# Four attention layers on one core: mixing constants added by ScalarE in PSUM, loads reordered, two results kept in PSUM

## The chip, the cores and the metric

The kernel runs on 1 core of one Trainium2 chip. The metric is the device time of one execution in microseconds (us), median of several runs, lower is better. The core has TensorE (PE, matmuls, results always in PSUM), VectorE (DVE), ScalarE (ACT), GpSimd (POOL) and SyncE (SP, which here only issues DMAs). In the profile PEld is TensorE's weight load, and "SPq", "DVEq" and the like are an engine's queue (issue, drains, waits) as against its datapath.

## What is computed

32 sequences of 64 tokens with 256 channels pass through four layers, all in f32. The reference, cut to its outline:

```python
x = L0(ctx, x, mask)       # attention of x over [ctx, x], 16 heads; rmsnorm; gelu MLP 256-1024-256
x = L1(x, state=ctx)       # layer norm, token shift, five mixes, linear recurrence over time, gated norm; then a second token-shift block
x = L2(x, ctx, masks)      # self attention, cross attention over ctx, gelu MLP 256-1024-256
x = L3(x, ctx, mask)       # cross attention over ctx, tanh(gate) * result added

# inside L1, the part the change touches
sx  = shift(xa) - xa
t   = tanh((xa + sx * maa_x) @ maa_w1)                  # five groups of 32 columns
m_j = t_j @ maa_w2[j]                                   # j = w, k, v, r, g
x_j = xa + sx * (maa_j + m_j)                           # the five mixes
...                                                     # r, k, v, g, decay from x_j; recurrence; y
y   = norm(y) * gn_w + gn_b;  x = x + (y * silu(g_proj)) @ Wo.T
x   = x + sigmoid(xr2 @ fWr.T) * (relu(xk2 @ fWk.T)**2 @ fWv.T)
```

## The kernel before, in words

The batch is cut into 8 groups of 4 sequences (256 tokens). A group lives in a "lane", one of four arenas in SBUF; lane i works through group i and then group i + 4. So four groups are under way at any time, each in one of the stages a (layer 0), b (first block of layer 1), c (second block of layer 1 and the self attention) and d (cross attention, MLP, layer 3). "First pass" below is groups 0 to 3, "second pass" groups 4 to 7.

Each engine runs one fixed instruction sequence. It is cut into steps, and the table `ORDER` says for each engine from which lane the next step comes: a string of digits, one digit a step (`P` is the prologue, on SP the loads of weights). A second table `BANKS` gives each PSUM tile one of the 8 banks. Both tables come from a planner outside the file. An engine never looks ahead: a step that waits blocks all that stands behind it.

The steps that matter here, with the lines of the kernel before:

- **Mixes** (`v_b`, line 993). For each of the five mixes PE fills a bank with t_j @ maa_w2[j] (line 622); DVE computes (bank + constant) * sx with two `scalar_tensor_tensor` instructions of 128x256, one for each half of the channels, into one of two slots of `L.mixed`; POOL adds xa (line 1482); PE runs the projection (lines 378 and 639). Mix n may overwrite its slot once projection n - 2 is done.
- **Recurrence** (`v_b`, `steps`): DVE multiplies in PSUM (line 1009), runs two scans (1013) and then a drain (1016) that hands the bank back; POOL multiplies by r (1492).
- **Gated norm** (lines 1057 and 1060): DVE multiplies the bank `rstd_rows` with `L.yc` in SBUF, result to SBUF, and hands the bank back at once; two more instructions of 128x256 read that result and make `L.yT`, on which PE waits (line 399).
- **End of layer 1** (lines 1083 and 1085): DVE computes (rr + 1) * bank `fv` into SBUF and hands the bank back, then adds half of it to x with an instruction of 128x512 whose two tensors both lie in SBUF.
- **Softmax of layer 0**: PE scores (543, 550), DVE maximum (940), ACT exp (1249), DVE sum and reciprocal (928, 930), POOL normalises (1420), PE transposes (366), ACT copies (1186), PE weights (571). POOL also makes the masks (1452), and adds the row constant to the residual x once x has been loaded (1458).
- **Loads**: SP issues, before anything else waits, the inputs of all four lanes, the weights `w_am`, the masks, the weights `w_b`, `w_c` and `w_d`, and only then the four residuals x (1566).

## Time and profile before

| what | value |
|---|---|
| median of 3 runs | 1033.16 us (1030.88 to 1034.33) |
| the profiled execution's own time | 1040.02 us |
| its span, first to last instruction | 1037.9 us |
| mean granted TensorE clock | 0.979 of full speed |
| busy: PE, DVE, ACT, POOL | 960.1, 742.7, 572.7, 543.3 us |
| weight loads of PE | 764.5 us |

The profiled execution took 6.9 us more than the median of the runs; all durations below are from that execution. Busy times are of one engine each and overlap freely. A matmul's end is modelled, so a busy PE is not a PE at its peak. "Idle before <- X" in a row is the time in which the engine stood still, put down to the instruction whose semaphore came last.

### The profile page before, as it was taken

Reading aid. Unit: us, or ns where it says so; the run is one execution under the profiler, and the core shown is the slowest. Engines: PE = TensorE matmul, PEld = TensorE weight load, DVE = VectorE, ACT = ScalarE, POOL = GpSimd, SP = SyncE. Lnnn points to the kernel's source line nnn. Section 1 sums busy time; section 2 is a strip of 40 time slices with the busy share of each in tenths; the row PEclk is TensorE's granted clock in tenths of the full one; section 3 lists DMA queues with packets and bytes.
Section 4 is the critical chain, followed back from the end, with each engine's and each line's share of the span. In section 5 each row is a group of like instructions: output and inputs, shape, how many; then the busy total and the mean of one; then the engine's idle time right before and its main releaser. Section 6 shows DMA issues by size and latency. Waiting matters only on the chain.

```text
span 1037.9 us, 27518 instructions
## 1 busy us (share of the span) xinstructions
PE 960.1 (92%) x10944; PEld 764.5 (74%) x10944; DVE 742.7 (72%) x1607; ACT 572.7 (55%) x1320; POOL 543.3 (52%) x662
## 2 busy tenths in 40 slices
PE   6979999989789999889999999998998999899997
PEld 4657886856567877668887788776767777688885
DVE  1485566788997788973756765676889887986675
ACT  2489733432333755667746587644545452575573
POOL 2364353574754456774426633555565664675341
PEclk9999999998897999999999999999999999999999
DMA  9601111000001001020101001101001000000001
GB/s 346 274 2 30 29 29 28 2 1 2 2 1 33 1 2 28 3 65 2 29 27 34 27 2 29 29 2 27 2 1 29 14 1 2 13 9 6 13 2 43
DMA packets 28589, 31.71 MB, mean 31 GB/s; under 512 B 14736, under 2 KB 25264, under 8 KB 27824
## 3 DMA queue, kind: packets, MB, share of 16 engines
q1 hardware_dynamic: 27440, 28.12, 8.4%
q8 instruction: 88, 1.44, 0.6%
q10 hardware_dynamic: 1024, 1.85, 0.5%
q14 instruction: 37, 0.30, 0.1%
HBM read 27.86 MB, written 2.10 MB: 29 GB/s over the span
## 4 chain that ended last, share of the span: by engine, by line
PE 53%; DVE 19%; DVEq 9%; issue 7%; ACT 5%; POOL 4%; POOLq 2%; DMA 1%; ACTq 0%; SPq 0%
PE bank L494 8%; PE bank L506 7%; PE bank L378 6%; PE bank L366 5%; PE bank L399 5%; PE bank L391 3%; DVE lane L1013 3%; DVEq L1016 3%; DVE bank L1009 2%; PE bank L457 2%; DVEq L886 2%; PE bank L481 2%; DVE lane L865 2%; PE bank L524 2%; PE bank L535 2%
## 5 line engine op out<-in xcount | busy, mean ns | idle before, releaser
L1420 POOL TENSOR_TENSOR lane<-lane 128x512 f32<-128x512 f32 x160 | 167.8, 1052 | 159.1 <-DVE lane L887 90.8
L1186 ACT COPY lane<-bank 128x512 f32<-128x512 f32 x232 | 132.0, 590 | 166.8 <-PE bank L366 103.9
L366 PE MATMUL bank<-ident,lane 128*128 128x128 f32 x896 | 131.9, 282 | 16.4 <-POOL lane L1420 4.5
L366 PEld LDWEIGHTS bank<-ident,lane 128*128 128x128 f32 x896 | 102.7, 143 | 42.8 <-issue 14.8
L1492 POOL TENSOR_TENSOR lane<-lane 128x512 f32<-128x512 f32 x64 | 81.3, 1271 | 70.1 <-DVE lane L1013 69.8
L1013 DVE TENSOR_TENSOR_SCAN lane<-lane,bank 128x256 f32<-128x256 f32 x128 | 80.9, 674 | 5.0 <-issue 0.4
L1205 ACT ACTIVATE lane<-lane 128x512 f32<-128x512 f32 x96 | 60.3, 633 | 28.9 <-DVE lane L865 28.5
L1154 ACT ACTIVATE lane<-lane 128x256 f32<-128x256 f32 x96 | 52.3, 594 | 42.4 <-POOL lane L1405 42.0
L885 DVE TENSOR_REDUCE lane<-lane 128x8 f32<-128x512 f32 x96 | 64.8, 675 | 12.1 <-ACT lane L1205 11.7
L1217 ACT ACTIVATE lane<-bank,vecs 128x256 f32<-128x256 f32 x128 | 51.9, 477 | 36.6 <-PE bank L494 36.3
L1168 ACT ACTIVATE lane<-bank,vecs 128x256 f32<-128x256 f32 x112 | 55.3, 550 | 22.9 <-PE bank L366 22.5
L1482 POOL TENSOR_TENSOR lane<-lane 128x512 f32<-128x512 f32 x40 | 46.8, 1180 | 39.2 <-DVE lane L993 39.2
L378 PE MATMUL bank<-lane,w_b 128*128 128x256 f32 x256 | 64.3, 398 | 2.9 <-POOL lane L1482 2.7
L506 PE MATMUL bank<-w_d,lane 128*128 128x256 f32 x256 | 61.6, 382 | 0.5 <-ACTq L1253 0.5
L506 PE MATMUL bank<-w_am,lane 128*128 128x256 f32 x256 | 61.2, 382 | 0.0
L494 PE MATMUL bank<-lane,w_d 128*128 128x256 f32 x256 | 59.1, 382 | 0.9 <-DVEq L1016 0.9
L494 PE MATMUL bank<-lane,w_am 128*128 128x256 f32 x256 | 58.8, 382 | 0.9 <-DVE lane L865 0.8
L378 PEld LDWEIGHTS bank<-lane,w_b 128*128 128x128 f32 x256 | 48.5, 197 | 14.2 <-POOL lane L1482 4.8
L816 DVE TENSOR_TENSOR lane<-bank,lane 128x512 f32<-128x512 f32 x48 | 33.0, 687 | 34.2 <-PE bank L399 23.8
L1179 ACT ACTIVATE lane<-bank,scalars 128x256 f32<-128x256 f32 x64 | 31.3, 540 | 46.3 <-PE bank L391 46.0
L1009 DVE TENSOR_TENSOR bank<-bank,lane 128x512 f32<-128x512 f32 x64 | 44.5, 695 | 17.1 <-PE bank L668 11.9
L494 PEld LDWEIGHTS bank<-lane,w_d 128*128 128x128 f32 x256 | 47.4, 190 | 8.5 <-DVEq L1016 1.3
(161 smaller groups left out, 2243.4 us busy)
## 6 DMA issues: line engine op xcount, KB each, us to landing
lane<-in_inT SPq DMA_DIRECT2D x16, 256.0 KB, 4.5
lane<-in_x SPq DMA_DIRECT2D x16, 256.0 KB, 2.9
w_d<-in_w_d SPq DMA_DIRECT2D x1, 3072.0 KB, 25.1
w_am<-in_w_am SPq DMA_DIRECT2D x1, 2048.0 KB, 15.5
lane<-in_inT SPq DMA_DIRECT2D x16, 128.0 KB, 3.0
lane<-in_ctx SPq DMA_DIRECT2D x8, 256.0 KB, 2.9
out_x<-lane SPq DMA_DIRECT2D x8, 256.0 KB, 2.2
w_c<-in_w_c SPq DMA_DIRECT2D x1, 1792.0 KB, 20.3
```

The lines of the kernel that those rows point to most:

```text
L366: ins = pe.transpose(t[:, i * P:(i + 1) * P], src, ident[:, :])
L378: ins = pe.matmul(o, w[:, ct, m * P:(m + 1) * P], r, start=(ct == 0), stop=(ct == CT - 1))
L494: ins = pe.matmul(t[:, i * T:(i + 1) * T], w1[:, ct, (2 * m + i) * P:(2 * m + i + 1) * P], xnT[:, ct, :], start=(ct == 0), stop=(ct == CT ...
L506: ins = pe.matmul(t[:, tt * C:(tt + 1) * C], hidden[k][:, tt * P:(tt + 1) * P], w2[:, k, :], start=(k == 0), stop=(k == FT - 1))
L885: v.tensor_reduce(A.den[:, j, :], grid(A.probs[j]), AX_X, ALU.add)
L1009: v.tensor_tensor(kv, kv, L.bk[:, m, :, 0:S].unsqueeze(1).to_broadcast([P, 2, G, S]), ALU.mult)
L1013: ins = v.tensor_tensor_scan(st[:, e, :, :].rearrange("p b t -> p (b t)"), w, bk.tile(key)[:, e * T:(e + 1) * T], 0.0, ALU.mult, ALU.add)
L1168: ins = s.activation(o, src, ACT.Identity, scale=vec(scale, ct), bias=vec(shift, ct) if shift else 0.0)
L1186: s.copy(out, src).then_inc(bk.free_sem(key), 1)
L1205: s.activation(A.probs[step], A.probs[step], ACT.Exp).then_inc(sig["probs"].sem, 1)
L1420: p.tensor_tensor(q, q, den.unsqueeze(2).to_broadcast([P, n, 512 // n]), ALU.mult).then_inc(sig["normal"].sem, 1)
L1492: p.tensor_tensor(st, st, L.br[:, m, :].unsqueeze(1).to_broadcast([P, 2, T]), ALU.mult).then_inc(sig["rs"].sem, 1)
```

## The change

**Mixes.** After PE has filled a mix's bank, ACT adds the constant in place: two `activation` instructions (Identity, with a bias per partition) of 128x256 that read and write the same bank. It signals a new semaphore `shares`. DVE waits for `shares` and multiplies the whole bank with sx in one `tensor_tensor` of 128x512. The POOL step and the projection stay as they are. ACT's steps for mixes 0 and 1 come ahead of its tanh of the decay projection, those of mixes 2 to 4 behind it, each a step of its own.

**Gated norm.** The product of `rstd_rows` and `L.yc` is written back into the bank; the two instructions that make `L.yT` read it there. The bank is handed back after them, by a drain that is new.

**End of layer 1.** (rr + 1) * `fv` is written back into the bank, the last instruction reads it there and hands the bank back.

**Loads.** The four residuals are issued ahead of the weights `w_am`, `w_b`, `w_c`, `w_d`. SP waits for all four residuals to have landed before it issues `w_b`; and by the new order it has by then also issued the second loads of x of lanes 1 and 0, each of which waits for that lane's norm of layer 0.

**Order and banks.** `ORDER` and `BANKS` are new throughout, on all engines. The semaphore `bias` is merged into `x_bias`.

```diff
@@ v_b, the mixes
                 if n >= 2:
                     v.wait_ge(bk.full_sem((g, "proj", MIXES[n - 2][0])), bk.full_at((g, "proj", MIXES[n - 2][0])))
-                for ct in range(CT):
-                    ins = v.scalar_tensor_tensor(L.mixed[:, (n + 1) % 2, ct, :], t[:, ct * T:(ct + 1) * T], vec(name, ct), L.sx[:, ct, :],
-                                                 ALU.add, ALU.mult)
-                ins.then_inc(bk.free_sem(key), 1)
+                v.wait_ge(sig["shares"].sem, sig["shares"].at(g, n + 1))
+                v.tensor_tensor(flat(L.mixed[:, (n + 1) % 2, :, :]), t[:, :], flat(L.sx[:, :, :]), ALU.mult).then_inc(bk.free_sem(key), 1)
@@ v_b, the gated norm
-            v.scalar_tensor_tensor(flat(L.yc[:, :, :]), bk.tile(key)[:, :], 0.5, flat(L.yc[:, :, :]), ALU.mult, ALU.mult).then_inc(bk.free_sem(key), 1)
+            t = bk.tile(key)[:, :]
+            v.scalar_tensor_tensor(t, t, 0.5, flat(L.yc[:, :, :]), ALU.mult, ALU.mult)
             v.drain()
             for m in range(CT):
-                ins = v.scalar_tensor_tensor(L.yT[:, m, :], L.yc[:, m, :], gnb_half[:, m:m + 1], L.gate[:, m, :], ALU.add, ALU.mult)
+                ins = v.scalar_tensor_tensor(L.yT[:, m, :], t[:, m * T:(m + 1) * T], gnb_half[:, m:m + 1], L.gate[:, m, :], ALU.add, ALU.mult)
             ins.then_inc(sig["yT"].sem, 1)
+            v.drain().then_inc(bk.free_sem(key), 1)
@@ v_c, the end of layer 1
-            v.scalar_tensor_tensor(flat(L.rr), flat(L.rr), 1.0, bk.tile(key)[:, :], ALU.add, ALU.mult).then_inc(bk.free_sem(key), 1)
+            t = bk.tile(key)[:, :]
+            v.scalar_tensor_tensor(t, flat(L.rr), 1.0, t, ALU.add, ALU.mult)
             v.drain()
-            v.scalar_tensor_tensor(flat(x[:, :, :]), flat(L.rr), 0.5, flat(x[:, :, :]), ALU.mult, ALU.add)
+            v.scalar_tensor_tensor(flat(x[:, :, :]), t, 0.5, flat(x[:, :, :]), ALU.mult, ALU.add).then_inc(bk.free_sem(key), 1)
@@ s_b
+            def share(n):
+                key = (g, "mix", MIXES[n][0])
+                s.wait_ge(bk.full_sem(key), bk.full_at(key))
+                t = bk.tile(key)
+                for ct in range(CT):
+                    ins = s.activation(t[:, ct * T:(ct + 1) * T], t[:, ct * T:(ct + 1) * T], ACT.Identity, bias=vec(MIXES[n][0], ct))
+                ins.then_inc(sig["shares"].sem, 1)
@@ sp_weights
             sp.dma_start(wt["am"][:, :], a["w_am"]).then_inc(load["am"].sem, 16)
             yield
+            for g in range(NL):
+                sp.wait_ge(lane(g).sig["x_loaded"].sem, lane(g).sig["x_loaded"].at(g, 1))
             sp.dma_start(wt["b"][:, :], a["w_b"]).then_inc(load["b"].sem, 16)
@@ ORDER
     "SP": (
-        "0123P0123PPP001122330123000000112202222331111213333302131203"
+        "0112021120023333P10P2PP3010210000111321021222333332301230123"
```

What SP issues first. Before, the weights `w_am`, `w_b` and the rest stand ahead of the residuals (`in_x`), the first of which is here:

```order
L1548 DMA lane3<-in_inT 128x512 x2
L1589 DMA w_am<-in_w_am 128x4096
L1560 DMA lane0<-in_mask0 128x256
L1560 DMA lane1<-in_mask0 128x256
L1560 DMA lane2<-in_mask0 128x256
L1560 DMA lane3<-in_mask0 128x256
L1591 DMA w_b<-in_w_b 128x3264
L1592 DMA lora_w2<-in_maa_w2g 32x256
L1594 DMA decay_w2<-in_decay_w2 64x256 x2
L1595 DMA consts<-in_consts 128x1028
L1597 DMA w_c<-in_w_c 128x3584
```

The change's SP, from the tenth DMA on (line numbers are the change's own):

```order
L1581 DMA lane0<-in_x 128x2x256
L1581 DMA lane2<-in_x 128x2x256
L1563 DMA lane3<-in_inT 128x512 x2
L1575 DMA lane3<-in_mask0 128x256
L1577 DMA lane3<-in_b_small 128x16
L1581 DMA lane3<-in_x 128x2x256
L1604 DMA w_am<-in_w_am 128x4096
L1584 DMA lane1<-in_x 128x2x256
```

So all residuals go out ahead of `w_am`, and `w_b` to `w_d` come after steps that wait for a norm. On PE the first 47 us of work are nearly the same in both orders: the queries, keys and values of all four lanes and the first scores of lanes 0 and 1 stand ahead of the first transpose (line 366) in either.

DVE, the mixes of group 0 in the kernel before (the last three of five, and what follows):

```order
L993 SCALAR_TENSOR_TENSOR lane0<-bank6,vecs,lane0 128x256 x2
L993 SCALAR_TENSOR_TENSOR lane0<-bank3,vecs,lane0 128x256 x2
L993 SCALAR_TENSOR_TENSOR lane0<-bank7,vecs,lane0 128x256 x2
L851 TENSOR_SCALAR lane3<-bank3,vecs 128x128
L816 TENSOR_TENSOR lane3<-bank2,lane3 128x512
```

The same place in the change:

```order
L851 TENSOR_SCALAR lane3<-bank7,vecs 128x128
L993 TENSOR_TENSOR lane0<-bank3,lane0 128x512
L940 TENSOR_REDUCE lane3<-bank4 128x4
L993 TENSOR_TENSOR lane0<-bank6,lane0 128x512
L993 TENSOR_TENSOR lane0<-bank2,lane0 128x512
L949 TENSOR_SCALAR lane2<-lane2 128x256 x2
```

Each pair has become one instruction, and here a softmax row of lane 3 has moved in between. On ACT the new rows of the same group (line 1287 of the change), between lane 3's softmax and the next steps of lane 0:

```order
L1276 ACTIVATE lane0<-bank1 128x256
L1277 ACTIVATE lane0<-bank1 32x256
L1280 ACTIVATE scalars<-scalars 128x1
L1287 ACTIVATE bank2<-bank2,vecs 128x256 x2
L1287 ACTIVATE bank6<-bank6,vecs 128x256 x2
L1250 ACTIVATE lane3<-bank7,lane3 128x128 x4
L1187 COPY lane3<-bank3 128x512
L1295 ACTIVATE lane0<-bank6 128x128
L1250 ACTIVATE lane3<-bank1,lane3 128x128 x4
L1259 ACTIVATE lane2<-lane2 128x256 x2
L1287 ACTIVATE bank3<-bank3,vecs 128x256 x2
L1287 ACTIVATE bank6<-bank6,vecs 128x256 x2
```

Behind the ACT rows of a mix stand exps and copies of other lanes, which wait with it.

Three counts from the orders that no short piece shows. ACT's table loads are 47 before and 45 in the change. Stage b of a pass, counted from the first lane's `maa_w1` matmul (line 607 before) to the last lane's matmul on `head_scale` (line 724 before), spans 882 PE instructions of 6017 in the first pass before and 946 in the change; in the second pass it spans 1872 before and 1162 in the change. On DVE the same stage of the second pass spans 535 of 1608 instructions before and 377 of 1568 in the change.

## Rows read from the trace of the kernel before

**Rows 1.** Page: busy us (share of span) and instructions.
```profile
PE 960.1 (92%) x10944; PEld 764.5 (74%) x10944; DVE 742.7 (72%) x1607; ACT 572.7 (55%) x1320; POOL 543.3 (52%) x662
```
**Rows 2.** Stretches: PE, PEld, DVE, ACT, POOL busy (count), granted clock, DMA share, GB/s.
```profile
0.00:50.00 50.00, 40.83 (x208) 28.52 (x208) 14.50 (x32) 18.89 (x42) 14.31 (x24) 1.00 0.85 321
50.00:90.00 40.00, 30.38 (x576) 24.98 (x577) 33.28 (x74) 34.79 (x109) 25.48 (x27) 0.96 0.09 21
200.00:350.00 150.00, 131.28 (x1166) 98.38 (x1165) 131.71 (x273) 55.52 (x105) 90.45 (x104) 0.90 0.02 7
450.00:700.00 250.00, 246.55 (x2726) 200.31 (x2727) 152.97 (x345) 161.05 (x410) 123.17 (x149) 1.00 0.08 22
700.00:900.00 200.00, 182.58 (x2053) 141.84 (x2052) 166.52 (x357) 100.12 (x237) 120.32 (x149) 0.98 0.04 10
```
**Rows 3.** Timeline of POOL, start and duration, with the idle before.
```profile
43.52 1.27 POOL L1458 TENSOR_TENSOR lane<-lane,rows 128x512 f32<-128x512 f32 x1 [15.44 <-DMA lane<-in_x]
44.74 2.04 POOL L1420 TENSOR_TENSOR lane<-lane 128x512 f32<-128x512 f32 x2
46.74 3.72 POOL L1458 TENSOR_TENSOR lane<-lane,rows 128x512 f32<-128x512 f32 x3
```
**Rows 4.** Stretch 47 to 56, columns as in rows 2.
```profile
47.00:56.00 9.00, 6.09 (x98) 4.86 (x96) 5.72 (x13) 6.33 (x22) 8.45 (x8) 1.00 0.01 3
```
**Rows 5.** Chain that ended last, 255 to 300: start, us, what.
```profile
264.24 0.57 DVEq L1058
...
268.73 0.69 DVE lane L1013
269.42 0.58 DVEq L1016
270.00 0.14 issue
270.13 1.66 DVE lane L993 x4
271.79 0.60 DVE lane L816
```
**Rows 6.** Groups of instructions: count, busy us, mean ns, idle before and its releasers.
```profile
L993 DVE SCALAR_TENSOR_TENSOR lane<-bank,vecs,lane 128x256 f32<-128x256 f32 x80 | 34.2, 478 | 24.6 <-PE bank L622 15.8 <-PE bank L378 8.6
L816 DVE TENSOR_TENSOR lane<-bank,lane 128x512 f32<-128x512 f32 x48 | 33.0, 687 | 34.2 <-PE bank L399 23.8 <-PE bank L506 9.8 <-issue 0.6
L1009 DVE TENSOR_TENSOR bank<-bank,lane 128x512 f32<-128x512 f32 x64 | 44.5, 695 | 17.1 <-PE bank L668 11.9 <-issue 4.1
L1083 DVE SCALAR_TENSOR_TENSOR lane<-lane,bank 128x512 f32<-128x512 f32 x8 | 5.5, 682 | 0.5 <-PE bank L399 0.3 <-issue 0.2
L1217 ACT ACTIVATE lane<-bank,vecs 128x256 f32<-128x256 f32 x128 | 51.9, 477 | 36.6 <-PE bank L494 36.3
L1168 ACT ACTIVATE lane<-bank,vecs 128x256 f32<-128x256 f32 x112 | 55.3, 550 | 22.9 <-PE bank L366 22.5
```
**Rows 7.** DVE busy in line 1085 alone, 200 to 350 and 700 to 900.
```profile
200.00:350.00 150.00, 1.59 (x2) 0.90 0.02 7
...
700.00:900.00 200.00, 3.27 (x3) 0.98 0.04 10
```
**Rows 8.** DVE busy in line 1060 alone, the same stretches.
```profile
200.00:350.00 150.00, 2.64 (x6) 0.90 0.02 7
...
700.00:900.00 200.00, 3.58 (x6) 0.98 0.04 10
```
**Rows 9.** Who PE waited for: us in total, times, longest.
```profile
PE bank L378 <- POOL lane L1482: 2.7, 6, 0.9
...
PE bank L639 <- POOL lane L1482: 1.2, 1, 1.2
```
**Rows 10.** Stretches of stage b, columns as in rows 2.
```profile
120.00:330.00 210.00, 189.45 (x1533) 142.65 (x1532) 163.45 (x329) 76.64 (x162) 113.31 (x126) 0.93 0.04 12
560.00:880.00 320.00, 304.50 (x3263) 240.26 (x3262) 239.88 (x519) 178.25 (x453) 177.57 (x213) 0.99 0.05 13
```

More of the change, by code:

```diff
@@ L118 @@
+        "222333333323333330110221102233033"
     ),
     "SP": (
[L120 removed]
+        "0112021120023333P10P2PP3010210000111321021222333332301230123"
     ),
@@ L1118, in v_d @@
             yield
-            v.wait_ge(sig["bias"].sem, sig["bias"].at(g, BIAS["m"]))
+            v.wait_ge(sig["x_bias"].sem, sig["x_bias"].at(g, BIAS["m"]))
             v_add_rows(v, (g, "mm", "rows"), x)
@@ L1280, in s_b @@
             yield
+            def share(n):
[5 more added lines that the diff above has]
+                ins.then_inc(sig["shares"].sem, 1)
+            for n in range(2):
+                share(n)
+                yield
             key = (g, "proj", "maa_w")
@@ L1284, in s_b @@
             yield
+            for n in range(2, 5):
+                share(n)
+                yield
             s_copy(s, (g, "proj", "maa_k"), L.bk[:, :, :, 1:S + 1].rearrange("p m b t -> p (m b) t"), grid(bk.tile((g, "proj", "maa_k"))[:, :]))
@@ L1412, in p_bias @@
             p.wait_ge(sig["normed"].sem, sig["normed"].at(g, NORM[tag]))
-            p.tensor_tensor(L.x, L.x, row(name).unsqueeze(1).to_broadcast([P, TT, C]), ALU.add).then_inc(sig["bias"].sem, 1)
+            p.tensor_tensor(L.x, L.x, row(name).unsqueeze(1).to_broadcast([P, TT, C]), ALU.add).then_inc(sig["x_bias"].sem, 1)
         def p_normal(p, g, tag, j, probs, den, n):
```

85 lines of the change are left out of this document (42 added, 43 removed).

## The prediction, made before the changed kernel was run

> **What bounds the kernel now.** I read the page's busy times first [rows 1]: PE is busy 960.1 of 1037.9 us and is idle for 77.8, and the change leaves its work alone. A gain can only come out of that idle time, or out of stretches in which PE ran at a lower granted clock. So the second view is the table of stretches [rows 2]. It shows three kinds. From 450 to 700 PE is busy 246.55 of 250 us with DVE at 153: PE alone is the bound, and nothing done to another engine helps there. From 200 to 350 PE is idle 18.7 of 150 us while DVE is busy 131.71 (88%) and PE's granted clock is down to 0.90; from 700 to 900 it is idle 17.4 of 200 with DVE at 166.52 (83%). There DVE sets the pace. From 50 to 90 PE is idle 9.6 of 40 us while ACT is busy 34.79 and DVE 33.28: the softmax of layer 0. The first 50 us hold another 9.2 us of idle, 7 of them before any data is there. The chain of waits inside 255 to 300 says the same of the second kind: DVE instructions and their drains follow each other with almost no PE between them [rows 5].
>
> **The loads.** POOL got its first residual at 43.5 us, after 15.44 us of waiting for it, and then had four residual additions and the normalisations queued behind them to work off [rows 3]. From 47 to 56 us it is the busiest engine, 8.45 of 9 us, and PE is idle 2.9 [rows 4]. With the residuals issued ahead of `w_am` and the later weights, POOL does this work while PE still computes keys and values. I take the 2.9 us of that stretch as saved. I don't take more, because PE's order up to its first transpose is nearly the same in both kernels, and from 56 us on ACT is the tight engine [rows 2], which this doesn't relieve. Bounds: zero, if ACT was late in that stretch anyway, and all the idle of the first 90 us but the first 7, 9.2 + 9.6 - 7 = 11.8 us. `w_b` now leaves SP only after the norm of layer 0 of lanes 1 and 0; the MLP of layer 0 and another norm stand between that and its first use, and the DMA engines carry 21 GB/s from 50 to 90 us against 321 in the first 50 [rows 2], so I take nothing for it. If that cover failed, PE's stage b and all behind it would stand. **Term 1: -2.9 us.**
>
> **DVE's work.** A mix costs two instructions of 478 ns [rows 6], which on the chain take 1.66 / 2 = 0.83 us for the pair [rows 5]. The one that replaces them has the shape and operands of line 816: 687 ns [rows 6], 0.60 on the chain [rows 5]. That is 2 x 478 - 687 = 269 ns saved in each of 40 mixes, 10.8 us in all; 10 mixes lie in each of the two DVE-bound stretches, so 5.4 us count. Line 1085 reads two tensors from SBUF and takes 1.59 + 3.27 = 4.86 us for five instructions there [rows 7]; with one operand in PSUM I price it like line 1083, 682 ns [rows 6], 3.41 for five: 1.5 us saved. Line 1060 takes 2.64 + 3.58 = 6.22 us for twelve [rows 8]; with a PSUM operand 12 x 478 = 5.74: 0.5 saved. Against it stands the new drain after `yT`. The drains on the chain cost 0.57 and 0.58 us [rows 5]; six of the eight fall into these stretches: 3.5 us. Net 5.4 + 1.5 + 0.5 - 3.5 = 3.9 us of DVE time. It counts whole if DVE is the chain there, which the stretch from 255 to 300 says, and not at all if PE's order waits for something else; without the drain's cost it would be 7.4. **Term 2: -3.9 us, bounds -7.4 and 0.**
>
> The two results kept in PSUM are now written there by VectorE. The nearest rows are lines 1009, which writes PSUM, 695 ns, and 816, which writes SBUF, 687 [rows 6]: 8 ns more for each of 16, 0.1 us, nothing. The Trainium skill (Advanced Engine Details and Errata, The Read-Write Bubble) says that VectorE lies closer to SBUF and ScalarE closer to PSUM; by it the two kept results would cost DVE more and ACT's additions less than a row that writes SBUF. For DVE the rows above show hardly a difference; for ACT no row here writes PSUM.
>
> **The mix's longer path.** ACT gets 80 instructions more. The nearest rows read PSUM and write SBUF with a bias per partition: 477 and 550 ns [rows 6], so 38 to 44 us, which takes ACT from 573 to about 615 busy (59%). Two table loads fewer hardly change it. ACT is not the bound outside the softmax of layer 0: it is busy 55.5 of 150 us from 200 to 350 [rows 2]. But the path from full bank to mixed tile grows from 0.83 + 0.1 to some 1.0 (ACT) + 0.69 (DVE), by 0.8 us. Behind the waiting ACT instruction stand exps and PSUM copies of other lanes, and behind the waiting DVE instruction that lane's POOL step and projection. PE waited for the POOL step seven times, 3.9 us in total [rows 9]. If each of these waits grew by 0.8 us it would cost 5.6; where a bank has stood full until DVE came to it, the cost is nothing. DVE stood idle for a bank ahead of line 993 for 24.6 us in all [rows 6], at 18 of its 80 instructions, so at most mixes the bank was full before DVE came. I take a quarter. **Term 3: +1.4 us, bounds 0 and +5.6.** Banks are held longer too (by 1 us a mix, by 1.2 for `rstd_rows`, 0.7 for `fv`). PE's waits for a bank to come free have no row of their own that would price this; with eight banks and a new bank table I take zero, and leave a microsecond or two of it to the range.
>
> **The sum.** Against the profiled execution's own time: 1040.0 - 2.9 - 3.9 + 1.4 = 1034.6 us. That execution stands 6.9 us above the median, a factor of 0.9934, which gives 1027.8, so 1028 us, 0.5% faster. The new order as a whole has no term: no row can price it. It is the largest unknown, and the rivals hold it.
>
> **Rival 1, the second pass is packed too densely (slower).** Before, stage b of the second pass spreads over 1872 PE instructions; in the change over 1162, near the 882 of the first pass before. DVE's heaviest work (the scans) then meets less PE work to hide behind. What that does can be read from the first pass: from 120 to 330 us PE is idle 20.6 us in 210 at clock 0.93; the second pass, 560 to 880, has only 15.5 us in 320 at 0.99 [rows 10]. If the second pass came to behave like the first, PE would idle 5.1 us more, and lose (0.07 x 210) - (0.01 x 320) = 11.5 us of clock, of which I count half, since PE is not always the bound: + 10.9 us, 1034.6 + 10.9 = 1045.5, in the median's scale 1039. With the whole clock loss it is 1044. It decides as soon as DVE's busy share in the second pass's stage b passes from the 83% of 700 to 900 to the 88% of 200 to 350. For it: the counts. Against it: PE instructions in the change's first pass are slightly more spread (946), and DVE has less to do.
>
> **Rival 2, the mixes come late.** Term 3 at its upper bound: 1034.6 + 4.2 = 1038.8, or 1032, no change that can be measured. For it: five mixes of a lane now pass through ACT in order between other lanes' softmax. Against it: ACT's low share in stage b.
>
> **Rival 3, the idle time opens up.** All of the start's 11.8 us come back instead of 2.9, and half of the clock loss of 200 to 350, (1 - 0.90) x 150 / 2 = 7.5 us: 1034.6 - 8.9 - 7.5 = 1018.2, or 1011. For it: POOL is 25 us earlier, and a relieved DVE keeps PE fed. Against it: ACT at 87% from 50 to 90, and a DVE relief of 3% in the stretches that matter.
>
> **How the numbers follow.** A measurement of this kernel tells about 0.3% from no change, that is below 1030.1 or above 1036.3. Forecast 0.43 (mostly faster, the rest within 0.3%), rival 1 0.26 (mostly slower), rival 2 0.14 (within), rival 3 0.17 (faster). From these: faster 0.31 + 0.17 = 0.48, same 0.10 + 0.13 + 0.03 = 0.26, slower 0.26. The range goes from 1012, rival 3's time, to 1043, near the upper end of rival 1.
>
> **What the profile after should show.** POOL's first addition to a residual before 25 us and no stretch of three in a row; PE idle of 47 to 56 us reduced by some 3. The `tensor_tensor` of the mixes near 690 ns, ACT's additions between 470 and 560, DVE's total near 742.7 - 10.8 - 4 = 728, ACT's near 613. PE's waits for the POOL step of the mixes at 5 us or so in total. In the second pass's stage b a DVE share at or below 85% and a granted clock near 0.98. The prediction is wrong if PE's busy time changes by more than 5 us (then it is the clock), if the idle time of the second pass grows, or if PE's total idle falls below 65 us.

## The result, and the profile after

The changed kernel takes 1042.2 us in the median of four executions (1040.5 to 1049.8), the kernel before 1032.9: a ratio of 1.0098, with a 95% interval from 1.0068 to 1.0127. The change made the kernel 1% **slower**. The forecast was 1028, with 1012 to 1043 as its range. (Two later kernels had one execution each of 1219 and 1240 us with a clock far below all others; they are left out of everything below, with the profile that belongs to the second.)

The changed kernel's profiled execution took 1043.5 us, its span is 1041.7. This first fence has the page's row of busy times and the stretches that answer to [rows 1] and [rows 2]; the columns are those of [rows 2].

```profile
PE 959.4 (92%) x10944; PEld 762.9 (73%) x10944; DVE 730.1 (70%) x1567; ACT 596.8 (57%) x1398; POOL 536.3 (51%) x662
...
0.00:50.00 50.00, 42.34 (x240) 29.29 (x240) 14.35 (x32) 19.06 (x42) 15.54 (x25) 1.00 0.44 154
50.00:90.00 40.00, 30.81 (x579) 25.07 (x575) 32.90 (x74) 32.83 (x104) 20.68 (x21) 0.91 0.01 2
200.00:350.00 150.00, 128.45 (x1177) 95.44 (x1176) 126.74 (x255) 62.39 (x126) 82.96 (x98) 0.93 0.01 3
450.00:700.00 250.00, 243.12 (x2848) 191.46 (x2847) 133.64 (x304) 176.42 (x507) 115.57 (x138) 1.00 0.11 30
700.00:900.00 200.00, 179.26 (x1938) 142.96 (x1937) 178.28 (x372) 100.17 (x201) 125.66 (x155) 0.97 0.02 7
```

PE's work is the same, 10944 instructions. Its idle time rose from 77.8 to 1041.7 - 959.4 = 82.3 us, though DVE has 12.6 us less to do. The gain is visible at the start (7.7 us idle in the first 50, before 9.2) and is given back later: 6.9 instead of 3.5 us from 450 to 700, and 20.7 instead of 17.4 from 700 to 900. There DVE's share went from 83% to 89%, while from 450 to 700 it fell from 61% to 53%. The new order puts DVE's work off.

The idle time explains 4.5 us; the medians lie 9 apart. The rest goes with the executions' granted clock. Over all executions of the kernels below that leave no work out and add none, the mean clock of a kernel lies between 0.986 and 0.989 with the order of before (the kernel before itself: 0.987), and between 0.975 and 0.979 with the new order. The profiled execution of before, at 0.979, was one of its slowest, which is why the two profiles stand only 3.8 us apart. At a like clock the two kernels hardly differ: of 110 executions of the kernel before that were taken beside the experiments below, the 8 at a clock from 0.978 to 0.980 took 1041.8 us on average. What this clock is worth is the subject of the last experiments.

The rows that answer to [rows 3], [rows 4] and [rows 10] follow: POOL's first residual addition, then the three stretches.

```profile
16.73 1.27 POOL L1473 TENSOR_TENSOR lane<-lane,rows 128x512 f32<-128x512 f32 x1 [1.12 <-DMA lane<-in_x]
```
```profile
47.00:56.00 9.00, 6.16 (x91) 4.75 (x90) 6.70 (x15) 6.39 (x20) 3.63 (x4) 0.87 0.01 3
120.00:330.00 210.00, 185.56 (x1589) 139.00 (x1588) 163.00 (x321) 94.64 (x215) 112.64 (x133) 0.95 0.11 38
560.00:880.00 320.00, 297.15 (x3048) 233.24 (x3050) 234.37 (x501) 177.30 (x444) 171.61 (x211) 0.98 0.05 15
```

POOL got its residual 27 us earlier and is busy 3.63 of the 9 us instead of 8.45, and yet PE is idle 2.8 us there, as before. In the second pass PE is idle 22.9 us instead of 15.5. What PE waited for from 47 to 56 us (us in total, times, longest), in the kernel before and in the changed one:

```profile
PE bank L543 <- ACT lane L1249: 1.4, 1, 1.4
PE bank L366 <- ACT lane L1249: 1.3, 2, 0.9
```
```profile
PE bank L571 <- ACT lane L1187: 0.8, 1, 0.8
PE bank L366 <- ACT lane L1187: 0.8, 1, 0.8
PE bank L543 <- ACT lane L1187: 0.8, 1, 0.8
```

Before, 2.7 of the 2.9 us were waits for ACT's exps and none for POOL. In the change they are waits for ACT's copies.

The groups that answer to [rows 6], [rows 7] and [rows 8] (mean duration of one in ns, then the idle time ahead and what ended it):

```profile
L993 DVE TENSOR_TENSOR lane<-bank,lane 128x512 f32<-128x512 f32 x40 | 27.1, 686 | 17.8 <-PE bank L378 9.3 <-ACT bank L1287 7.2 <-issue 1.1
L1059 DVE SCALAR_TENSOR_TENSOR lane<-bank,scalars,lane 128x256 f32<-128x256 f32 x16 | 7.0, 479 | 0.7
L1086 DVE SCALAR_TENSOR_TENSOR lane<-bank,lane 128x512 f32<-128x512 f32 x8 | 5.5, 691 | 0.6
L1084 DVE SCALAR_TENSOR_TENSOR bank<-lane,bank 128x512 f32<-128x512 f32 x8 | 5.5, 687 | 0.4 <-issue 0.4
...
L1287 ACT ACTIVATE bank<-bank,vecs 128x256 f32<-128x256 f32 x80 | 31.1, 457 | 15.2 <-PE bank L622 15.0
```

Who PE waited for: of the whole span the two largest on other lanes' norms, the one on the constants, and the one on a mix's POOL step, which answers to [rows 9].

```profile
PE bank L366 <- ACT lane L1155: 9.0, 7, 2.4
PE bank L724 <- DVE lane L1049: 5.8, 4, 3.6
PE bank L366 <- DMA consts<-in_consts: 1.8, 1, 1.8
PE bank L639 <- POOL lane L1497: 0.2, 1, 0.2
```

### The profile page after: what moved, and what is told of

Read it like the earlier page. It is cut to its first block, busy times and chain, and to the rows that moved or that the text cites. A ratio compares the mean times of both kernels' runs of the same rounds, so it can differ in the third digit from the quotient of the medians.

```text
span 1041.7 us, 27582 instructions
## 1 busy us (share of the span) xinstructions
PE 959.4 (92%) x10944; PEld 762.9 (73%) x10944; DVE 730.1 (70%) x1567; ACT 596.8 (57%) x1398; POOL 536.3 (51%) x662
## 4 chain that ended last, share of the span: by engine, by line
PE 54%; DVE 16%; ACT 6%; POOL 6%; DVEq 6%; issue 6%; POOLq 2%; DMA 1%; SPq 1%; ACTq 1%
PE bank L506 7%; PE bank L366 7%; PE bank L494 7%; PE bank L378 6%; PE bank L399 5%; PE bank L391 4%; DVE lane L1011 3%; PE bank L457 3%; DVEq L1014 3%; DVE bank L1007 3%; PE bank L481 3%; PE bank L524 2%; PE bank L535 2%; POOL lane L1507 2%; PE bank L438 2%
## 5 line engine op out<-in xcount | busy, mean ns | idle before, releaser
L366 PE MATMUL bank<-ident,lane 128*128 128x128 f32 x896 | 136.8, 287 | 27.6 <-ACT lane L1155 9.0
L366 PEld LDWEIGHTS bank<-ident,lane 128*128 128x128 f32 x896 | 105.4, 146 | 55.2 <-issue 22.5
L378 PE MATMUL bank<-lane,w_b 128*128 128x256 f32 x256 | 61.6, 386 | 1.0 <-ACT lane L1308 0.4
L940 DVE TENSOR_REDUCE lane<-bank 128x4 f32<-128x512 f32 x64 | 42.8, 672 | 18.7 <-PE bank L550 18.6
L494 PEld LDWEIGHTS bank<-lane,w_d 128*128 128x128 f32 x256 | 47.7, 190 | 10.8 <-ACT lane L1169 2.6
L378 PEld LDWEIGHTS bank<-lane,w_b 128*128 128x128 f32 x256 | 46.8, 190 | 10.8 <-issue 4.8
L494 PEld LDWEIGHTS bank<-lane,w_am 128*128 128x128 f32 x256 | 47.6, 190 | 8.6 <-issue 1.4
```

The costliest lines, as they stand in the source:

```text
L366: ins = pe.transpose(t[:, i * P:(i + 1) * P], src, ident[:, :])
L378: ins = pe.matmul(o, w[:, ct, m * P:(m + 1) * P], r, start=(ct == 0), stop=(ct == CT - 1))
L494: ins = pe.matmul(t[:, i * T:(i + 1) * T], w1[:, ct, (2 * m + i) * P:(2 * m + i + 1) * P], xnT[:, ct, :], start=(ct == 0), stop=(ct == CT ...
```

## The experiments

Ratios are to the kernel before, run beside each kernel on the same chip, with 95% intervals. In the diffs, a minus line is the kernel named, a plus line the experiment.

### The new order alone

The changed kernel with the mixes, the two results and the loads taken back; ORDER and BANKS are the new ones. The share steps of ACT stay as empty steps:

```diff
-                share(n)
-                yield
+                yield
```

> The changed kernel with its three edits in code taken back (the mixes as two fused DVE instructions, no steps of ACT for them; both results written to SBUF; the loads in the order of before), so that only the new order of the engines and the new bank table are left. Theory A (the order itself is what costs: the second pass's stage b is packed too densely): the time stays 8 to 14 us above the kernel before, 1041 to 1047, since the edits' own gain is missing too; DVE's busy share from 700 to 900 us is 89% or more and PE is idle 20 us or more there. Theory B (the longer way of a mix through ACT and DVE costs it): 1030 to 1035, and the idle time of 700 to 900 falls back to about 17.4 us. Theory C (w_b and the constants come late): about 1036 to 1038, with the wait of 1.8 us on the constants gone and the clock of 90 to 120 us back.

Measured: 1051.9 us, ratio **1.0152** (1.0113 to 1.0191), mean clock 0.975. So with the old code the new order costs 1.5%, some 16 us, and the three edits together give back 0.5%, 5.6 us (1.0098 against 1.0152; each ratio has an interval of 0.3 to 0.4% on either side). That is theory A in kind and more than the whole result; the time lies 5 us above the range that theory A gave. Of the 15.1 us by which this kernel's span exceeds that of before (1053.0 against 1037.9), 10.6 are idle time of PE (88.4 against 77.8), 8.0 of them after 450 us; the other 4.5 are PE's busy time, at a clock of 0.972 against 0.979. The new order has its steps placed for the changed code and runs here without it, so the 1.5% is not the order's price inside the change. Stretches 450 to 700 and 700 to 900 of this kernel:

```profile
450.00:700.00 250.00, 243.10 (x2815) 192.32 (x2814) 140.00 (x326) 166.00 (x469) 116.61 (x141) 1.00 0.11 30
700.00:900.00 200.00, 177.65 (x1802) 139.76 (x1803) 174.40 (x366) 92.03 (x195) 119.80 (x149) 0.95 0.03 7
```

DVE's share from 700 to 900 is 87% (theory A had 89 or more), PE is idle 22.4 us there. The scans (line 1013) show what the order does in the second pass. The first fence is the kernel before, DVE's busy time in that line for stretches of 50 us with the count in brackets, the second the new order alone:

```profile
550.00:600.00 50.00, 10.12 (x16) 1.00 0.11 32
600.00:650.00 50.00, 0.00 (x0) 1.00 0.06 16
650.00:700.00 50.00, 7.57 (x12) 1.00 0.06 16
700.00:750.00 50.00, 5.08 (x9) 0.95 0.07 15
750.00:800.00 50.00, 7.59 (x12) 0.98 0.06 16
800.00:850.00 50.00, 5.06 (x8) 1.00 0.03 8
```
```profile
600.00:650.00 50.00, 5.06 (x8) 1.00 0.15 40
650.00:700.00 50.00, 5.06 (x8) 1.00 0.06 15
700.00:750.00 50.00, 15.58 (x25) 1.00 0.06 16
750.00:800.00 50.00, 4.65 (x8) 0.90 0.01 1
800.00:850.00 50.00, 10.12 (x16) 1.00 0.00 1
```

Before, they are spread from 550 on, never more than 16 in 50 us; in the new order none runs before 600, and 25 fall between 700 and 750.

### One edit at a time on the kernel before

**The mixes.** The five steps of ACT for each lane's mixes are put into the order of before at the places where that trace shows the mix's bank full (the signals of three biases were merged with another to free semaphores):

```diff
-                for ct in range(CT):
-                    ins = v.scalar_tensor_tensor(L.mixed[:, (n + 1) % 2, ct, :], t[:, ct * T:(ct + 1) * T], vec(name, ct), L.sx[:, ct, :],
-                                                 ALU.add, ALU.mult)
-                ins.then_inc(bk.free_sem(key), 1)
+                v.wait_ge(sig["shares"].sem, sig["shares"].at(g, n + 1))
+                v.tensor_tensor(flat(L.mixed[:, (n + 1) % 2, :, :]), t[:, :], flat(L.sx[:, :, :]), ALU.mult).then_inc(bk.free_sem(key), 1)
```

> The kernel before with only the mixes changed: ACT adds the constants in PSUM, DVE multiplies once; ACT's order gets 40 steps more, everything else keeps its order. Theory A: the edit is worth what the prediction's sum gave it, -5.4 for DVE and +1.4 for the longer way, so 1028 to 1031, at most equal to before. Theory B: PE's waits for the mixes grow by 5 us or more in total and the time is 1036 to 1041. DVE's busy time falls by 10 to 12 us in both, ACT's rises by 40 to 45.

Measured: 1039.7 us, ratio 1.0033 (1.0012 to 1.0055). The edit costs 3 us here instead of bringing 4. DVE's busy time fell from 742.7 to 733.4, by 9.3, and ACT's rose by 28.2 (572.7 to 600.9) where 40 to 45 were expected. The mix's group and three waits of PE in this kernel:

```profile
L993 DVE TENSOR_TENSOR lane<-bank,lane 128x512 f32<-128x512 f32 x40 | 27.2, 687 | 31.9 <-ACT bank L1284 26.0 <-PE bank L378 4.0 <-issue 1.7
```
```profile
PE bank L366 <- ACT lane L1152: 6.1, 8, 1.3
...
PE bank L378 <- POOL lane L1494: 3.6, 6, 1.3
...
PE bank L639 <- POOL lane L1494: 1.6, 2, 1.2
```

DVE stands 26.0 us waiting for ACT's additions, and its idle time ahead of the mixes grew from 24.6 us [rows 6] to 31.9: by 7.3, most of what it saved. PE's waits for the mix's POOL step grew from 3.9 us [rows 9] to 5.2, by the 1.3 us that term 3 had as 1.4; the larger part came elsewhere, PE's waits for ACT's work for other lanes (line 1152, line 1154 before) went from 4.0 to 6.1. ACT has 80 additions more to get through. So the time is theory B's, but not by its mechanism, waits for the mixes that grow by 5 us or more.

**The two results in PSUM**, with the drain after `yT`, in the order of before:

```diff
-            v.scalar_tensor_tensor(flat(L.rr), flat(L.rr), 1.0, bk.tile(key)[:, :], ALU.add, ALU.mult).then_inc(bk.free_sem(key), 1)
+            t = bk.tile(key)[:, :]
+            v.scalar_tensor_tensor(t, flat(L.rr), 1.0, t, ALU.add, ALU.mult)
```

> The kernel before with only the two results kept in PSUM and the drain after yT. The prediction's working gives -1.5 -0.5 +3.5 = +1.5 us: 1034, within 0.3% of before. If the drains cost nothing beside other work it is 1031. A third theory, that banks held 1.2 and 0.7 us longer make PE wait for a free bank, would show as 2 to 6 us more (1036 to 1040).

Measured: 1035.3 us, ratio 0.9978 (0.9953 to 1.0004); DVE 737.7 us. The interval goes from 4.9 us gained to 0.4 lost, so a gain is not shown, but the sum's +1.5 lies outside it. If the rest of the edit is worth what the sum gave it, the drains' 3.5 us are not there; no kernel has the drain alone.

**The loads as in the change**: masks and residuals first, `w_b`, `w_c` and `w_d` behind the norms. The wait for the residuals ahead of `w_b` is taken over too. In SyncE's order a digit is a lane's next step (the fifth waits for its norm of layer 0), P is the next weight:

```diff
-        "0123P0123PPP001122330123
+        "0112021120023333P01P2PP3
```

> The kernel before with only SyncE's order of the first loads changed: masks and residuals ahead of w_am, and w_b, w_c and w_d one after another only behind the norms of layer 0 (here of lane 0 and lane 1, in this order, since the order of before needs lane 0 first). Term 1 of the prediction gives -2.9 us, 1030. Theory C gives +1 to +4, 1034 to 1038, with a wait of PE's first stage b for the constants near 100 to 115 us. Theory A says that this edit decides nothing: within 3 us of before.

Measured: 1039.1 us, ratio 1.0043 (1.0020 to 1.0067), theory C. What PE waited for from 90 to 120 us:

```profile
PE bank L366 <- DMA consts<-in_consts: 3.6, 1, 3.6
```

**The loads without the late weights**: the same, but all weights directly behind the residuals.

```diff
-        "0123P0123PPP001122330123
+        "0112021120023333PPPP0123
```

> The kernel before with the masks and residuals ahead of all weights, but with w_am, w_b, w_c and w_d issued right behind them, before any wait for a norm, so that POOL gets its residuals early and no weight is late. Term 1 of the prediction: -2.9 us, ratio 0.997. If ACT is late in 47 to 56 us anyway, as the profile of the changed kernel suggests: 1.000, with PE idle near 2.9 us in that stretch as before. If w_am is what comes late instead: PE idle for it before 40 us and 1.002 or more.

Measured: 1034.0 us, ratio **0.9959** (0.9941 to 0.9977). The size is near what term 1 said (0.997 lies in the interval), but the reason that it gave does not show. Its stretch from 47 to 56:

```profile
47.00:56.00 9.00, 5.76 (x97) 4.50 (x95) 6.52 (x14) 7.29 (x25) 4.55 (x5) 1.00 0.01 3
```

PE is idle 3.2 us there, no less than before. Its total idle time is not less either (1029.9 - 949.1 = 80.8 us); PE's busy time is, at a clock of 0.991. Where the gain arises the profile doesn't show.

### One edit undone in the changed kernel

The edits of the diffs above in reverse, order and banks as changed (the mixes with ACT's steps empty).

> The changed kernel with the mixes taken back to two fused DVE instructions each; order, banks, loads and the two results in PSUM stay. If the mixes' edit is worth in the new order what the sum gave it (-5.4 +1.4 = -4.0), this runs 4 us longer than the changed kernel, a ratio to the kernel before of 1.013 to 1.015. If DVE is the tight engine in a second pass packed too densely, the whole 10.8 us of DVE work counts for more: 1.016 to 1.020. If the edit costs in this order what it cost on the kernel before (+0.33%), the ratio is 1.005 to 1.007.

Measured: ratio 1.0100 (1.0072 to 1.0128), against 1.0098 of the changed kernel: in the new order no worth of the mixes' edit shows. The difference of the two is known to 0.4% only. The interval ends just below the 1.013 that the sum's 4 us would give, and a cost of 0.33% as in the old order is not excluded.

> The changed kernel with the two results written to SBUF again and without the drain after yT. The prediction gave the edit +1.5 us, so a ratio to the kernel before of about 1.008; on the kernel before the edit measured -0.22%, by which this is 1.012. Nothing else should move: DVE's busy time up by 4 to 5 us.

Measured: 1050.3 us, ratio 1.0123 (1.0099 to 1.0148): a difference of 0.25% to the changed kernel, the same sign and size as the 0.22% on the kernel before. Neither is clear of its interval. DVE's busy time is up by 6.8 us (736.9 against 730.1).

> The changed kernel with SyncE's first 24 steps and their wait as before: the weights ahead of the masks and residuals. Term 1 says that this loses 2.9 us, a ratio to the kernel before of 1.0125. The run on the kernel before (+0.43% for the late weights) says that it gains about 4 us, 1.005 to 1.006, with PE's wait for the constants near 113 us gone. Theory A (the new order's dense second pass costs the most) is touched by neither: the idle time from 700 to 900 us stays above 20 us.

Measured: ratio 1.0106 (1.0078 to 1.0133). The edit as it stands is worth 0.1%, not told from nothing. PE is idle 19.9 us from 700 to 900, the wait for the constants is gone. That two effects cancel here is what the next one suggests, where only the lateness of the weights is taken away:

> The changed kernel with w_b, w_c and w_d issued behind w_am and the residuals, before the norms. If the late weights cost in the new order what they cost on the kernel before (0.43% + 0.41% between late and early), the ratio falls from 1.010 to 1.002. If only the wait of 1.8 us and the 1.8 us of idle from 90 to 120 us come back, 1.006 to 1.008. If the new order was made for the late loads and a lane waits for something else, no change.

Measured: 1041.8 us, ratio 1.0054 (1.0029 to 1.0080). The wait for the constants is gone, and 0.4% comes back (known to 0.4% either way against the changed kernel; against the one with the loads undone it is 0.5%). So the late `w_b` costs some 4 us in this order, by the middle values more than the 1.8 us of its wait.

### What in the order costs: three probes

Each probe takes work of the second groups away from one engine, in the kernel before and in the kernel with the new order alone. An engine that sets the pace in one order and not in the other should give back more there, unless another engine stands right behind it. The new order alone is known to 0.4% (4 us), and so are its probes, so a difference between the two orders' gains below some 6 us can't be seen.

DVE's product ahead of the scans, for two time steps of each batch only:

```diff
-                v.tensor_tensor(kv, kv, L.bk[:, m, :, 0:S].unsqueeze(1).to_broadcast([P, 2, G, S]), ALU.mult)
+                few = S if g < NL else 2
+                v.tensor_tensor(kv[:, :, :, 0:few], kv[:, :, :, 0:few], L.bk[:, m, :, 0:few].unsqueeze(1).to_broadcast([P, 2, G, few]), ALU.mult)
```

> A probe of how much the end depends on DVE in the second pass's stage b, on the kernel before. In lanes' second groups VectorE's multiplication by k ahead of the scans (line 1009, 695 ns) is done for the first two time steps of each batch only, so the output isn't the reference's; 32 instructions shrink, about 17 us of DVE's work go, and every wait and signal stays. In this order the stages b of the second pass stand one after another (550-600, 661-719, 722-776, 818-867 us in the trace): DVE is the bound only in part of that time, and 5 to 9 us come back, a ratio of 0.991 to 0.995.

> The same probe on the kernel with the new order alone (the three edits in code taken back). Theory A (the three stages b lie over each other, 605-683, 665-749 and 694-770 us, and DVE sets the pace there): the time falls by 12 to 17 us, from 1.015 to 1.000 to 1.004, at least twice as much as on the kernel before. If the density is not what costs and the new order loses its time elsewhere (waits of PE in softmax and MLP, the clock), it falls as much as there, 5 to 9 us, to 1.007 to 1.010.

Measured: 0.9920 (0.9892 to 0.9947) and 1.0086 (1.0055 to 1.0118, against 1.0152). The order of before gives back 0.8%, the new one 0.7%. With 7 us, known to 5 either way, the new order doesn't give back the 12 to 17 of theory A. The scans' density, which rival 1 named, is there, but as far as this probe tells it is not what sets the two apart.

DVE's sums of the probabilities replaced by a constant:

```diff
-                v.tensor_reduce(A.den[:, j, :], grid(A.probs[j]), AX_X, ALU.add)
+                if g >= NL and tag != "l3":
+                    v.memset(A.den[:, j, :], 64.0)
+                else:
+                    v.tensor_reduce(A.den[:, j, :], grid(A.probs[j]), AX_X, ALU.add)
```

> A second probe on the kernel before: in the second groups VectorE's sums of the probabilities in the self and cross attentions (line 885, 675 ns) are replaced by a constant, so the output isn't the reference's; 32 instructions shrink, some 18 us of DVE's work, as much as in the first probe but in the attentions. The first probe gave 8 us here and 7 with the new order, so the scans' density is not what sets the two orders apart. Theory A2 (the new order puts the attentions of three lanes on DVE at once, from 725 to 900 us, where it is busy 156 of 175): 5 to 8 us come back here, ratio 0.992 to 0.995. Theory P (POOL's order): the same here.

> The second probe on the kernel with the new order alone. Theory A2: DVE's late pile of attention work is what costs, so 13 to 18 us come back, from 1.015 to 0.998 to 1.003. Theory P (what costs is that PE waits for normalisations whose POOL steps stand behind other lanes' POOL steps): no more than on the kernel before, 5 to 8 us, 1.007 to 1.010. If both stay at that, DVE work of either kind is worth the same in both orders, and the cost lies in how the order interleaves, not in one engine's work.

Measured: 0.9971 (0.9950 to 0.9992) and 1.0112 (1.0075 to 1.0150): 0.3% and 0.4%, less than either theory had in either order. Theory A2 falls.

POOL's product with r, for four elements only (`st[:, :, 0:few]` in place of `st`):

> A third probe on the kernel before: in the second groups POOL's multiplication of the scanned states by r (line 1492 of the kernel before, 1276 ns) is done for four elements only, so the output isn't the reference's; 32 instructions shrink, some 35 us of POOL's work in the second pass. POOL waited for DVE 52 to 69 us ahead of these. Theory A2: 0 to 2 us, ratio 0.998 to 1.000. Theory P: 2 to 5 us, 0.995 to 0.998.

> The third probe on the kernel with the new order alone. Theory P: PE's waits for the normalisations (7.3 us against 3.0 from 600 to 900 us) shrink to half or less and 6 to 12 us come back, from 1.015 to 1.004 to 1.009. Theory A2: 0 to 3 us, 1.012 to 1.015.

Measured: 1.0003 (0.9980 to 1.0026) and 1.0153 (1.0122 to 1.0184). POOL is busy 504.9 us instead of 539.1 and nothing came back. Theory P falls.

### Is it the clock? Filling PE's waits

In the changed kernel with early weights the deepest fall of the second pass stands at 840 us. The first fence is that kernel from 840 to 860, the second the same stretch with the filler:

```profile
840.00:860.00 20.00, 15.15 (x186) 12.65 (x187) 18.75 (x38) 9.19 (x18) 11.50 (x13) 0.74 0.01 1
```
```profile
840.00:860.00 20.00, 17.54 (x231) 14.72 (x218) 17.79 (x41) 7.96 (x15) 10.76 (x14) 0.91 0.01 2
```

DVE is busy 18.75 of the 20 us; PE had been idle 2.4 us at one wait for ACT and 2.2 at one for DVE. The filler, ahead of the named steps of PE:

```diff
-        next(streams[stage])
+        if fill is not None and k in FILL:
+            fill(FILL[k])
+        next(streams[stage])
...
+            def fill(n):
+                i = int("".join(BANKS)[sum(bk.fills)])
+                pe.wait_ge(bk.free[i], bk.frees[i])
+                for _ in range(n):
+                    pe.matmul(bk.bank[i][:, 0:256], ident[:, :], wt["a"][:, 0:256], start=True, stop=True)
```

> The changed kernel with the weights issued early (as in the run before of that name, ratio 1.0054, mean granted clock 0.979 against 0.987 of the kernel before), and with 35 matmuls of 0.47 us that compute nothing of use ahead of 16 steps of PE in the second pass, where the trace shows PE idle for 0.7 to 2.4 us, each into the bank that the step opens next; 16.5 us of filling in all for 19 us of idle time. Theory clock (what the new order costs is largely that idle time gathers in few places, after which PE's granted clock falls, as at 840 us to 0.61): the clock of 840 to 860 us stays near 1, the mean clock rises by 0.004 or more and the time falls by 2 to 5 us, 1.001 to 1.004. Theory idle (the waits themselves cost, the clock follows for free): filling gives nothing back and delays some steps, +0 to +4 us, 1.005 to 1.009.

Measured: 1042.2 us, ratio 1.0064 (1.0042 to 1.0085), mean clock 0.986 instead of 0.979. The clock is back and the time is not.

> The same, with 40 more such matmuls ahead of 20 steps of PE from 240 to 550 us, where the trace shows low clocks at 240 (0.58) and 290 (0.83). Theory clock: the mean clock rises by 0.008 or more, to the 0.987 of the kernel before, and the time falls by 4 to 9 us, 0.997 to 1.002. Theory idle: +0 to +8 us, 1.005 to 1.013.

Measured: 1048.4 us, ratio 1.0115 (1.0081 to 1.0150), at a mean clock of 0.990, the highest of all. Both results look like theory idle, but the traces show that the filler doesn't separate the two theories. It waits for the bank that it writes, so part of it runs behind PE's wait and not in it. At the deepest place, with the filler of the second pass:

```profile
842.77 3.30 PE L808 MATMUL bank<-w_a,ident 128*128 128x256 f32 x8 [2.46 <-DVE lane L862]
845.86 1.02 PE L371 MATMUL bank<-ident,lane 128*128 128x128 f32 x4
```

The 2.46 us of waiting are still there, the 3.30 us of filling follow them, and the step behind then doesn't wait. All filling of that kernel (20.3 us, where 16.5 were expected), then of the one with both passes; the number behind the bar is the busy time, the one behind the mean is the waiting ahead of the filling:

```profile
L808 PE MATMUL bank<-w_a,ident 128*128 128x256 f32 x70 | 20.3, 420 | 4.8 <-DVE lane L862 2.5 <-ACT lane L1180 0.9 <-DVEq L1025 0.9
```
```profile
L808 PE MATMUL bank<-w_a,ident 128*128 128x256 f32 x150 | 46.3, 439 | 15.5 <-DVE lane L862 3.5 <-DVEq L1025 3.3 <-ACT lane L1198 2.9
```

Without filler PE is busy 958.2 us and idle 83.8. With the first one its busy time without the filling is 967.3 - 20.3 = 947.0, and idle time and filling together are 71.6 + 20.3 = 91.9; with the second they are 941.2 and 106.3. So at the higher clock (0.988 and 0.986 in these two profiles, 0.980 without filler) PE's own work took up to 11.2 and 17.0 us less, and filling and idle time took 8.1 and 22.5 us more. (Both are upper values, since the filling and the step behind it overlap a little in the profile.) How much of the less would have reached the end without the filling is not shown. At a like clock the changed kernel with early weights (0.979, 1041.8 us) takes what the kernel before takes at 0.978 to 0.980, while the new order alone (0.975, 1051.9) lies 8 us above the one execution of before at 0.974 (1043.6). So idle time and the lower clock both look like parts of the cost, and no run here separates them.

The stretch from 600 to 1000 shows that idle time. It is, in turn, the kernel before, the new order alone, the changed kernel, and the changed kernel with early weights and the filler:

```profile
600.00:1000.00 400.00, 379.75 (x4318) 307.25 (x4317) 305.42 (x663) 232.03 (x531) 219.22 (x274) 0.99 0.05 12
```
```profile
600.00:1000.00 400.00, 373.82 (x4192) 298.50 (x4192) 305.02 (x661) 213.65 (x489) 228.33 (x279) 0.97 0.05 13
```
```profile
600.00:1000.00 400.00, 375.64 (x4216) 301.76 (x4213) 307.10 (x658) 235.04 (x542) 229.76 (x282) 0.98 0.04 10
```
```profile
600.00:1000.00 400.00, 387.32 (x4276) 310.53 (x4275) 307.36 (x659) 232.70 (x537) 229.74 (x282) 1.00 0.04 10
```

DVE does the same work in these 400 us in all four, 305 to 307 us. PE is idle 20.3, 26.2 and 24.4 us in the first three. The fourth's idle time, 12.7 us, is less only by its filler.

### A version that beats both

> The kernel before with two parts of the change and none of its order: the residuals early with no late weights, and the two results kept in PSUM. Both alone measured 0.9959 and 0.9978; if they add, 0.994, about 1031 where before takes 1037.

Measured: 1031.6 us, ratio 0.9968 (0.9947 to 0.9989). It beats both kernels, and so does the one with the early loads alone (0.9959); the two effects don't add visibly. It also gives a second price of the order: it differs from the changed kernel with early weights (1.0054) by the order, the banks and the mixes' edit, and these three cost 0.9% together. The best use of this change is its loads, with the weights not late, in the old order.

## Why the prediction was wrong

**The sum left out the term that decided.** The step that failed is the sentence "The new order as a whole has no term: no row can price it." It put the order at nothing. With the old code the order costs 1.5%, 16 us, against a sum of edits of 5.4. Inside the change its price is smaller and less well known: the three edits measured +0.33, -0.22 and +0.43% one by one on the kernel before, +0.5% if they add, while in the new order they take off 0.5%. Against edits that add to +0.5%, the order would account for only 0.4 of the 1.0%; the kernel before with all three edits was not run. With early weights the order, the banks and the mixes' edit cost 0.9% (1.0054 against 0.9968). So the order costs 1.5% with the old code, 0.9% with early weights and the results in PSUM (the mixes' edit included), and perhaps as little as 0.4% with all edits; and the edits that were to gain 0.5% don't gain it in the old order.

The prediction saw the order as a danger and gave rival 1 a chance of 0.26. Its rival had rows for a price, so one did exist: the idle time and the clock of the first pass [rows 10]. Rival 1 gave 1039, and up to 1044 with the whole clock loss; measured were 1042. Its condition held, DVE's share from 700 to 900 rose to 89%, and so did its idle time (+5.1 forecast; 20.3 to 24.4 from 600 to 1000, 15.5 to 22.9 from 560 to 880), which the prediction had named as a sign of being wrong; and the mean clock fell from 0.987 to 0.978. Its mechanism is not shown: work taken off DVE there pays no more in the new order than in the old one, within some 6 us. The clock loss that it counted, 5.75 us, is neither confirmed nor refuted by the filler.

**Term 1, the loads (-2.9).** Two steps. "I take the 2.9 us of that stretch as saved" was wrong in place: POOL was the busiest engine there, but PE's waits of before were for ACT's exps (2.7 of 2.9 us), which the kernel before's own trace shows. POOL's backlog went, and ACT was late as before, as the lower bound had it (2.8 us idle after; 3.2 with the early loads on the kernel before). And "so I take nothing for it" was wrong on `w_b`: the cover didn't reach. PE waited 1.8 us for the constants in the changed kernel and 3.6 in the order of before, and late against early weights is 0.4% in the new order (1.0098 against 1.0054) and 0.8% in the old (1.0043 against 0.9959). The constants are issued last in that step, behind `w_b`, and are the first that is used. As a whole the term measures -0.1% in the new order.

**Term 2, DVE's work (-3.9).** The durations of single instructions were right: 686 ns for the mix's product (687 taken), 479 for line 1059 (478), 691 for line 1086 (682), 730.1 us of DVE in all (728). The saving was not: two instructions of a pair overlap (80 x 478 ns are 38.2 us, and the group is busy 34.2 [rows 6]), so the mixes' rows fell by 34.2 - 27.1 = 7.1 us and not by 10.8, and 5.4 in the two stretches should have been 3.6. What it is worth was not either: the mixes' edit, -5.4 of this term and +1.4 of the next, shows no worth in the new order and costs 0.33% in the old. DVE's saving became waiting there (7.3 us more ahead of the mixes); its waits for ACT's additions are 26.0 us in the old order and 7.2 in the new one. The results in PSUM, +1.5 in the sum, measure -0.2% on either order, not clear of nothing but clear of +1.5 on the kernel before: the six drains don't seem to cost the 0.58 us each that the chain's rows showed for others.

**Term 3, the mix's longer path (+1.4).** PE's waits for the mix's POOL step grew by 1.3 us in the order of before, as counted, and nearly vanished in the changed kernel (0.2 us). What it didn't count is that ACT's additions delay ACT's work for other lanes (+2.1 us of PE's waits on line 1154). ACT's busy time in the changed kernel is 596.8 us and not some 613: the additions overlap too (80 x 457 ns are 36.6 us, busy 31.1). The additions write PSUM and take 457 ns, less than the 477 and 550 of the rows that write SBUF, as the prediction's sentence from the Trainium skill (Advanced Engine Details and Errata, The Read-Write Bubble) would have it for ScalarE; the rows differ in more than where they write, so this agrees with the page and doesn't prove it.

**The scale.** The profiled execution of before was 7 us above its median at a clock of 0.979. The factor 0.9934 carried that to the forecast, but the changed kernel's executions lie at that lower clock as a rule (0.978 on average). Of the 14.4 us between 1027.8 and 1042.2 this is a large part: against the profiled executions' own times, 1034.6 forecast and 1043.5 measured, the error is 8.9 us.

**What stays open.** That the new order costs is shown, and that PE's idle time grows with it, mostly after 450 us. Which of its moves does it is not: DVE's scans, DVE's sums and POOL's products, each taken alone and within some 6 us, don't account for the difference, and two engines at once were not tried. How much of the cost is idle time itself and how much the lower clock that goes with it is open too, and so is the order's price beside all three edits. A kernel with the first pass of one order and the second of the other could tell more and was not run: the lanes end their first pass at other times in the two orders.

## What to carry to other kernels

When a change rewrites the order of a kernel, don't put the order at nothing: give it a term from the nearest rows, and measure the new order with the old code first. A stage that spreads over fewer instructions of the bound engine (1872 to 1162 here) was a warning that came true, in this one case, though the mechanism behind it was not confirmed. Before a stretch's idle time is counted as saved, ask the trace whom the bound engine waits for there; the busiest engine need not be the one. A saved instruction is worth what its engine's next wait leaves of it, so ask who hands over the operand now. When loads are moved forward, follow what is moved back, down to the last DMA of the step.

## What the runs showed of the hardware

- Putting matmuls of no use into PE's sequence raised the mean granted clock from 0.979 to 0.986 and 0.990, and the time not at all or the wrong way (1.0054 to 1.0064 and 1.0115). PE's own work took up to 11.2 and 17.0 us less, but the filling took 20.3 and 46.3 us, part of it behind the waits (4.8 and 15.5 us of waiting stood ahead of the filling itself). A filler should be judged by what it takes as well as by the clock.
- Among executions of one kernel the time goes with the clock: of 110 executions of the kernel before, the 8 at a clock from 0.978 to 0.980 took 1041.8 us on average and the 30 from 0.990 to 0.993 took 1033.4. Two profiles should be compared only with their clocks beside them.
- ScalarE with a bias per partition, reading and writing PSUM, took 454 to 458 ns for 128x256, against 477 and 550 for the lines that write SBUF. VectorE took 687 and 693 ns for the two 128x512 results in PSUM, against 682 and 681 for the same lines writing SBUF.
